# An attention and gated feed-forward block on one core: a projection's weights, a batch's values, and the third batch's turning and keys are done at other places in the slot order

## What is computed

```python
q = heads(concat([ssm_states, hidden], -1) @ Wq, 32)
k, v = heads(hidden @ Wk, 8), heads(hidden @ Wv, 8)
ssm_k, ssm_v = heads(ssm_states @ Wsk, 8), heads(ssm_states @ Wsv, 8)
scores = q @ concat([rep(ssm_k), rep(k)]).T / sqrt(16) + alibi
scores = where(window of 64 keys back, scores, -inf)
o = softmax(scores) @ concat([rep(ssm_v), rep(v)])
return o @ Wo
```

## Time and profile before

| | us |
|---|---|
| median of 3 runs | 875.04 (873.82 to 875.11) |
| the profiled execution | 874.93 |
| its span | 871.9 |
| PE busy, share of the span | 862.1 (99%) |
| DVE busy | 545.9 (63%) |
| ACT busy | 400.6 (46%) |
| POOL busy | 519.5 (60%) |

### The profile page before, as it was taken

The page is one execution under the profiler, slowest core; times in us unless marked ns, Lnnn a source line. Parts: engine busy times, 40 slices in busy tenths (PEclk is TensorE's granted clock), DMA queues, the critical chain, the costliest instruction groups (busy, mean ns, idle before and its releaser), DMA issues.

```text
span 871.9 us, 17392 instructions
## 1 busy us (share of the span) xinstructions
PE 862.1 (99%) x6662; PEld 754.0 (86%) x6662; DVE 545.9 (63%) x983; ACT 400.6 (46%) x810; POOL 519.5 (60%) x532
## 2 busy tenths in 40 slices
PE   9999999999999999999999999999999999999998
PEld 8889999999999999988888868888888888888886
DVE  7675666776666657755436746556655665565567
ACT  5754555554545545654034243444444444444431
POOL 3861443534335232353769998547888888788731
PEclk9999999999999999999999999999999999999999
DMA  8677576776868659630101345311212021121046
GB/s 275 170 142 185 149 200 192 188 197 162 210 164 219 164 138 261 140 98 26 49 24 53 106 147 163 139 50 48 72 50 73 25 72 56 42 73 48 1 137 249
DMA packets 76459, 108.07 MB, mean 124 GB/s; under 512 B 7249, under 2 KB 47954, under 8 KB 75346
## 3 DMA queue, kind: packets, MB, share of 16 engines
q1 hardware_dynamic: 74168, 105.94, 43.2%
q10 hardware_dynamic: 2210, 1.03, 0.4%
HBM read 70.71 MB, written 31.00 MB: 117 GB/s over the span
## 4 chain that ended last, share of the span: by engine, by line
PE 94%; DVE 2%; DMA 1%; issue 1%; ACT 0%; SPq 0%; DVEq 0%; ACTq 0%
PE ps_scores L2219 20%; PE ps_proj L1840 16%; PE ps_scoresT L2219 10%; PE ps_scoresT L1977 7%; PE ps_o L1991 6%; PE ps_proj L1829 6%; PE ps_scores L1950 5%; PE ps_scores L1840 5%; PE ps_proj L2219 5%; PE ps_proj L1898 5%; PE ps_scoresT L1840 4%; DMA xn_rows<-in_x 1%; PE ps_o_max L2018 1%; PE ps_o L1829 1%; PE ps_o_max L1829 1%; PE ps_o_max L1878 1%
## 5 line engine op out<-in xcount | busy, mean ns | idle before, releaser
L1127 ACT ACTIVATE probsT<-ps_scoresT 128x512 f32<-128x512 f32 (+1 forms) x256 | 138.9, 545 | 148.6 <-PE ps_scoresT L1977 144.1
L1485 DVE TENSOR_REDUCE neg_max<-ps_scores 128x2 f32<-128x384 f32 (+1 forms) x256 | 131.7, 517 | 108.1 <-PE ps_scores L1950 107.4
L1352 ACT ACTIVATE part_sums<-ps_scores 128x512 f32<-128x512 f32 x96 | 57.4, 598 | 132.5 <-PE ps_scores L2219 130.5
L1977 PE MATMUL ps_scoresT<-q_stack,k_stack 116*128 116x256 f32 x448 | 106.1, 307 | 0.0
L840 POOL TENSOR_TENSOR o_normal<-o_blocks,inv_sums 128x256 f32<-128x256 f32 x32 | 19.9, 622 | 137.0 <-DVE inv_sums L1506 137.0
L1950 PE MATMUL ps_scores<-k_stack,q_stack 114*128 114x192 f32 (+1 forms) x512 | 94.6, 267 | 2.9 <-DMA q_stack<-qT_hi 1.4
L1950 PEld LDWEIGHTS ps_scores<-k_stack,q_stack 114*128 114x128 f32 x512 | 83.0, 190 | 9.8 <-DMA q_stack<-qT_hi 2.0
L995 POOL TENSOR_TENSOR w_expert_lo<-w_sums,w_expert_hi 128x256 fp32r<-128x256 f32 x64 | 63.8, 1008 | 45.5 <-ACT w_expert_hi L1276 45.5
L1007 POOL TENSOR_TENSOR big<-big,basis 128x512 f32<-128x512 f32 x56 | 77.9, 1409 | 16.3 <-DVE basis L1779 16.3
L1977 PEld LDWEIGHTS ps_scoresT<-q_stack,k_stack 116*128 116x128 f32 x448 | 70.8, 190 | 3.8
L1770 DVE TENSOR_TENSOR basis<-part_sums,silu_gate 128x512 f32<-128x512 f32 x32 | 24.2, 756 | 67.3 <-ACT silu_gate L1360 67.3
(11 more groups left out here) (311 smaller groups left out, 2507.5 us busy)
## 6 DMA issues: line engine op xcount, KB each, us to landing
k_stack<-k_kept SPq DMA_DIRECT2D x64, 192.0 KB, 4.5
big<-coeff_rows SPq DMA_DIRECT2D x8, 1024.0 KB, 4.6
q_stack<-q_kept SPq DMA_DIRECT2D x40, 192.0 KB, 4.1
q_kept<-qT_hi SPq DMA_DIRECT2D x10, 512.0 KB
x_rows<-in_x SPq DMA_DIRECT2D x9, 512.0 KB, 6.6
k_kept<-kT_hi SPq DMA_DIRECT2D x16, 256.0 KB
x_kept<-x_rows SPq DMA_DIRECT2D x16, 256.0 KB, 2.8
w_raw<-in_L_ffn_w_gate SPq DMA_DIRECT2D x16, 256.0 KB, 2.9
```

The lines of the kernel that those rows point to most:

```text
L1127: act.activation(PT[:, g % 2, 2 * j:2 * j + blocks].rearrange("p h f r w -> p (h f r w)"), ST[:, n % 2, 0:blocks].rearrange("p h n -> p (h ...
L1352: act.activation(TP[:, u % 2, j, :], src[:, u % 2, :], ACT.Copy).then_inc(taken, 1)
L1485: dve.tensor_reduce(NM[:, g // 2 % 2, g % 2, 2 * i:2 * i + 2], SA[:, n % 2, :, 0:keys], AX.X, ALU.max, negate=True).then_inc(max_done, 1)
L1977: ins = pe.matmul(ST[:, n % 2, v, :], KS[0:ROWS, g, j + v, 1 - v].rearrange("p w s -> p (w s)"), QS[0:ROWS, g, j + v].rearrange("p f r w - ...
```

## The change

Output weights: SP loads the four quarters two by two, behind the stacks of the sixth head (number 5) and of the seventh (number 6), and the split goes from slots 12 to 15 to slots 18 to 21. The second batch's values go from 20, 21, 22 to 15, 16, 17. Of the third batch, the high halves of the context go from 22 and 23 to 19 and 20, the low ones from 28 to 22, turning from 23 and 27 to 20 and 22, keys from 31, 32, 33 to 24, 25, 28. Its row statistics go before slot 0 and its normalising to 14. The high part of the second batch's first queries is taken between two of ACT's `rows_out`, the low part in slot 2 in place of 8. The load of ACT's Exp table goes from before the slots to slot 11.

```diff
-EARLY_Q = ((-1, -1, 7), (-1, -1, 8), (9, 10, 11), (12, 13, 14))
+EARLY_Q = ((-1, -1, 1), (-1, -1, 8), (9, 10, 11), (12, 13, 14))
-EARLY_STATS = (11, 13)
+EARLY_NORMAL = 14
+EARLY_V, EARLY_PREP, EARLY_K, EARLY_CTX_HIGH = (15, 16, 17), (20, 22), (24, 25, 28), (19, 20)
-SPLIT_WO = 12
+SPLIT_WO, WO_AFTER = 18, {5: (0, 1), 6: (2, 3)}
+EARLY_CTX_LOW = 22
+EXP_TABLE = 11
...
+def early_due(n, early, usual, first, after=0):
+    if n == early + after:
+        return first
+    return due(n, usual + after, first + 1)
...
+def values_due(n, part, after=0):
+    return early_due(n, EARLY_V[part], V_PROJ[part], 1, after)
...
         keep_k(0)
-        for n in range(FIRST_O, len(halves)):
-            weight(n)
         for g in range(HK):
             stack_k(0, g)
             stack_q_first(g)
+            for n in WO_AFTER.get(g, ()):
+                weight(FIRST_O + n)
...
         k_high(1)
         rows_out(4)
+        q_high(1, 0)
         rows_out(6)
-        table_of(ACT.Exp)
...
+        for t in range(TB):
+            row_stats(2, t)
         for n in range(SLOTS):
```

More of the change, by code:

```diff
@@ L117, in queries_due, with normal_due, prep_due, keys_due @@
     return due(n, Q_PROJ[r][part] + after, 2)
-def stats_due(n, t):
-    return 2 if n == EARLY_STATS[t] else due(n, STATS[t], 3)
+def normal_due(n):
+    return 2 if n == EARLY_NORMAL else due(n, STATS[1] + 1, 3)
+def early_due(n, early, usual, first, after=0):
[4 more added lines that the diff above has]
+    return early_due(n, EARLY_V[part], V_PROJ[part], 1, after)
+def prep_due(n, t, after=0):
+    return early_due(n, EARLY_PREP[t], PREP[t], 2, after)
+def keys_due(n, part, after=0):
+    return early_due(n, EARLY_K[part], K_PROJ[part], 2, after)
+def ctx_low_due(n, j):
+    return 2 if n == EARLY_CTX_LOW else due(n, CTX_LOW[j], 3)
 def pair_due(n, offset):
@@ L197, in projections @@
     for n in range(SLOTS):
-        jobs = [("k", due(n, K_PROJ[0], 2), 0)] + [("q", queries_due(n, i, 0), i) for i in range(G)]
-        jobs += [("v", due(n, V_PROJ[0], 1), 0)]
+        jobs = [("k", keys_due(n, 0), 0)] + [("q", queries_due(n, i, 0), i) for i in range(G)]
+        jobs += [("v", values_due(n, 0), 0)]
         jobs += [("wo", batch_at(n, lambda b: wo_slots(b, t)[0]), t) for t in range(TB)]
@@ L209, in turns @@
     for n in range(SLOTS):
-        jobs = [("prep", due(n, PREP[t], 2), t) for t in range(TB)] + [("turn_v", due(n, TURN_V), 0)]
+        jobs = [("prep", prep_due(n, t), t) for t in range(TB)] + [("turn_v", due(n, TURN_V), 0)]
         jobs += [("x", batch_at(n, lambda b: x_turn_slot(b, t)), t) for t in range(TB)]
@@ L912, in _ @@
             for j in range(2):
-                b = due(n, CTX_LOW[j], 2)
+                b = ctx_low_due(n, j)
                 if b is not None:
                     ctx_low(b, j)
-            b = stats_due(n - 1, 1)
+            b = normal_due(n)
             if b is not None:
@@ L1209, in _ @@
             for i in range(2):
-                b = due(n, CTX_HIGH[i], 2)
+                b = early_due(n, EARLY_CTX_HIGH[i], CTX_HIGH[i], 2)
                 if b is not None:
                     ctx_high(b, i)
-                b = due(n, PREP[i] + 1, 2)
+                b = prep_due(n, i, 1)
                 if b is not None:
                     prep_high(b, i)
-            b = due(n, K_PROJ[2] + 1, 2)
+            b = keys_due(n, 2, 1)
             if b is not None:
@@ L1220, in _ @@
                 b = queries_due(n, i, 2, 1)
-                if b is not None:
+                if b is not None and (b > 1 or i > 0):
                     q_high(b, i)
+            if n == EXP_TABLE:
+                table_of(ACT.Exp)
             for t in range(TB):
@@ L1607, in _ @@
             for t in range(TB):
-                b = due(n, PREP[t] + 1, 2)
+                b = prep_due(n, t, 1)
                 if b is not None:
                     prep_low(b, t)
-            b = due(n, K_PROJ[2] + 1, 2)
+            b = keys_due(n, 2, 1)
             if b is not None:
@@ L1617, in _ @@
                     q_low(b, i)
-            b = due(n, V_PROJ[2] + 1, 1)
+            b = values_due(n, 2, 1)
             if b is not None:
@@ L1636, in _ @@
             for t in range(TB):
-                b = stats_due(n, t)
+                b = due(n, STATS[t], 3)
                 if b is not None:
@@ L2111, in _ @@
             for t in range(TB):
-                b = due(n, PREP[t], 2)
+                b = prep_due(n, t)
                 if b is not None:
@@ L2124, in _ @@
             for part in range(3):
-                b = due(n, K_PROJ[part], 2)
+                b = keys_due(n, part)
                 if b is not None:
@@ L2131, in _ @@
                         queries(b, r, part)
-                b = due(n, V_PROJ[part], 1)
+                b = values_due(n, part)
                 if b is not None:
```

## The result

The changed kernel takes 878.49 us (median of 14 executions, 876.97 to 885.19), the kernel before 875.25 us (14 executions, 873.45 to 878.5). The ratio is 1.0036, with a 95% interval of 1.0020 to 1.0052: slower by 0.36%, outside the forecast range, on the side to which I gave 0.22. The profiled execution took 878.26 us with a span of 875.4 us (874.93 and 871.9 before).

What follows compares the result with a forecast made beforehand. TensorE, 99% busy, bounds the kernel; only idle time before 70 us can change. Of 3.1 us won up to slot 18, 2.9 are given back in Scalar's and POOL's queues: gain 0.2, median 874.8 us, range 872.9 to 877.0.

Steps and rivals of the forecast that it cites:

- the start and the filled slots: Slots 0 to 18: earlier stacks 1.3 us, slot 9's wait gone 0.45, values in slots 15 to 17 1.35.
- I took 1.3: First stack load: lands 1.3 us earlier, bounds 0 to 2.0, with the weight loads no longer beside the keys' write.
- The rival that they land no earlier: Slot 0's stacks: the keys' write is not held up by the weights, 1.3 us less won, 876.0; no separate chance.
- its reading of the rule on how a write is spread over the DMA engines: Keys' write: spread over 8 of sixteen engines, so weights behind it hardly hold it up; the 1.3 us would be 0.
- the chain through Scalar, VectorE and POOL: Slots 18 to 24: Scalar tight, TensorE waiting for VectorE and POOL; 2.9 of 3.1 us won given back, nearly all there.
- about 2: Slot 24: the first key third waits for both context halves on POOL, about 2 us of TensorE's time.
- The slower rival: Third weight load 0.8 to 2 us late stops Scalar's in-order queue, shifting Exps and keys: 876.7 to 878, chance 0.22.
- the 0.2 us that I took for a late load: Third weight on Scalar: load at 55.6, wanted at 54.8, 0.8 us late; 0.2 us taken, moving slot 32 to 68.6.
- the four loads' long issue came from full rings: SP: the loads' 4.14 us issue blamed on full rings at the start, so 2.2 us taken at the new place.
- the second batch's stacks are not the bound: Slot 32: SP's chain frees it at 67.8 (66.8 to 70), before the 68.6 of the other chain.
- I had left 0.8 in slots 29 to 31: Slots 29 to 31 have no filler, so 0.8 of the present 1.0 us of waiting for row maxima stays.
- its end at 60.7 plus slot 25 with a third (1.5), slot 26 with the value product (2.15) …: Slots 24 to 28: from the first key third's end at 60.7, slots 25 to 28 summed to 66.2.

Runs made afterwards that it cites:

- e1: The changed kernel with only the output weights' part undone (loads ahead of the first stacks, split in slots 12 to 15): 875.44 us, ratio to before 0.9998.
- e5: The kernel before with only the second batch's values moved to slots 15 to 17: 874.62 us, ratio to before 0.9990.
- e10: The changed kernel with weights, turning, keys and context halves as before; early values and first queries' low part stay: 874.40 us, ratio 0.9990.
- e6: The changed kernel with the output weights split in slots 21 to 24 instead of 18 to 21: 875.84 us, ratio to before 1.0002.
- e9: The changed kernel with weight splits in slots 21 to 24 and both low context halves in slot 21, ahead of them on POOL: 874.54 us.
- e2: The changed kernel with 32 unused products added where TensorE waits, in slots 20, 22 and 24: 877.16 us, ratio to before 1.0028.
- e8: e6 with the third batch's key thirds in slots 25, 29 and 31 instead of 24, 25 and 28: 876.28 us, ratio to before 1.0011.
- e3: The kernel before with only the output weights' part (loads behind sixth and seventh heads, split in slots 18 to 21): 877.73 us, ratio 1.0025.

## Why the prediction was wrong, point by point

The places of the sum against the trace, 0.68 us taken off the measured ones:

| place | forecast | measured |
|---|---|---|
| first stack load behind the keys' write | 7.5 | 7.1 (28.12 − 21.02) |
| turn in slot 20 | 53.5 | 53.4 |
| third weight split on Scalar | 54.8, load 0.8 late | 54.8, load in time |
| turn in slot 22 | 56.5 | 56.7 |
| first key third in slot 24 | 59.7 (60.7 less 0.96) | 59.6 |
| both context halves done on POOL | 60.4 | 60.6 |
| second keys written | 52.9 | 53.6 |
| slot 32 | 68.6 | 71.3 |
| slot 34 | 69.6 | 72.4 |

- **Right: the start and the filled slots.** No wait at 9 and 17. The stacks started 1.7 us earlier behind the write than before (8.78 to 7.10), where I took 1.3. In the four profiles with the weights behind the write (before, e1, e5, e10) it is 8.74 to 8.81, in all others 7.06 to 7.14. The rival that they land no earlier fell, and with it its reading of the rule on how a write is spread over the DMA engines: the weights behind it held its landing up.
- **Right: the chain through Scalar, VectorE and POOL.** Every place up to slot 24 came within 0.2 us, and TensorE waited there for what I had named. One reading in it was off: the key third began with the first half of the context and not with both, so that the wait was 1.24 us and not "about 2"; the start that the sum used, 59.7, fits only this. The slower rival's mechanism, Scalar stopped by a load, didn't occur: in the changed kernel Scalar's operations followed each other within 0.1 us from 51.78 to 59.6, and the 0.2 us that I took for a late load were not needed. That the four loads' long issue came from full rings no run shows; at their new place the pairs took 1.05 us each on SP.
- **Right: the second batch's stacks are not the bound.** Slot 32 waited 0.76 us for VectorE's maxima, of which I had left 0.8 in slots 29 to 31.
- **Wrong: "its end at 60.7 plus slot 25 with a third (1.5), slot 26 with the value product (2.15) …".** These terms came from the earlier trace rows, where TensorE has 2.4 GHz. I had put three waits, in slots 20, 22 and 24, into the sum, counted each once, as idle time, and took the durations behind them from rows that stand behind no such waits. What the lower level cost is read from e6, which has the same order on TensorE and kept 1.00: the starts of the scores in slots 25, 26 and 27, first in the changed kernel, then in e6.

```profile
62.09 0.57 PE L1984 MATMUL ps_scores<-k_stack,q_stack 114*128 114x192 f32 x2
...
64.60 0.57 PE L1984 MATMUL ps_scores<-k_stack,q_stack 114*128 114x192 f32 x2
...
67.34 0.37 PE L1984 MATMUL ps_scores<-k_stack,q_stack 114*128 114x192 f32 x2
```

```profile
60.24 0.37 PE L1984 MATMUL ps_scores<-k_stack,q_stack 114*128 114x192 f32 x2
...
61.63 0.37 PE L1984 MATMUL ps_scores<-k_stack,q_stack 114*128 114x192 f32 x2
...
63.94 0.37 PE L1984 MATMUL ps_scores<-k_stack,q_stack 114*128 114x192 f32 x2
```

| stretch | forecast | e6, at 1.00 | the change |
|---|---|---|---|
| third in slot 24 | 0.96 | 1.04 (estimate: eight matmuls and a restart) | 1.84 |
| slot 25 | 1.5 | 1.39 | 2.51 |
| slot 26 | 2.15 | 2.31 | 2.74 |
| slots 27 and 28 | 1.92 | 2.14 | 2.15 |
| slots 29 to 31, with the wait at 32 | 2.2 | 2.51 | 2.50 |
| slots 32 and 33 | 0.95 | 1.13 | 1.12 |

  Slot 34 is 2.8 us late against the forecast (72.4 and 69.6). The clock made 2.4 of it, in the first three rows. The other terms were 0.8 short at any clock, most of it in slots 26 and 28 to 31; the load that was not late and a start of the third 0.1 earlier took 0.3 to 0.4 back.
- **In the median it is larger.** The forecast was 874.8, measured 878.49, 3.7 more; all 14 executions had 0.996 or less, 7 of them less than the profiled one's 0.996. Their mean clocks average 0.9946, which is 4.7 us of 875 if every lost cycle counts; at the profiled execution's rate (2.4 us lost where 6.8 us at 0.50 make 3.4) it is 3.3, an estimate. How much of the 3.7 is the clock's and how much are waits that vary can't be told apart further in executions without a trace. e9, which removes the wait of slot 24 and cuts that of slot 22 from 1.23 to 0.65, gives back 3.9.
- **The chances.** I gave the slower side 0.22 on a mechanism that did not happen. The profile of before showed no drop of the clock at all, so there was no row to price one; but the sum itself showed three waits within 8 us. A price for TensorE at the lower level from the first of them to the end of the last (53.5 to 60.7), half of 7.2 us, would have given 878.4. That it meets the measured time is luck: the drop that came lay elsewhere, from 58.1 to 64.9 on the same scale, so the stretch of the waits is no bound for it. The range should have gone beyond 877.0, by an amount that no row of before could give.

The Trainium skill (TensorE: Matmul & The Clock Gate, "HAM oscillation — how this bites in real kernels") describes waits after which the clock is at half rate, and puts the price at the throttled time times one half. By it the 6.8 us here cost 3.4 us. The rows give 2.4. For one thing, 1.2 us of the stretch was the wait of slot 24, in which there was nothing to slow down, and by the same rule the 5.56 busy us cost 2.8. For another, the projection matmuls stood 0.21 us apart, not twice 0.12. The trace agrees in kind, and the page's price is an upper end here.

## What to carry to other kernels

When a sum puts several waits on TensorE close together, price the matmuls behind them at the lower clock too, and look at the row of the granted clock before looking for a cause elsewhere. When work is moved into an in-order queue, write down the order in every queue that it passes: here it decided between 878.5 and 874.5 us whether the four weight splits stood ahead of the context halves in Scalar's and POOL's queues or behind them, and the DMA transfers, to which much of the forecast's text went, were not the loss. Filler products in front of a wait are a cheap test of whether the waits bring the clock down, if the same number of them is also run where TensorE doesn't wait; count the executions that keep the clock, since the times of the two also differ by what the idle time hides.

## What the runs showed of the hardware

**The clock fell at a wait pattern, not at a wait.** The longest wait ahead of the drop was 1.23 us, with TensorE busy 6.21 of 8.80 us; the wait of slot 24 came behind it. e2's profiled execution had one of 1.84 us and kept 1.00 there. e1's fell at 38.0, behind a wait of 2.0 us for the first stacks. e6 was busy only 5.99 of the same 8.80 us:

```profile
50.00:58.80 8.80, 5.99 (x50) 5.41 (x48) 6.52 (x13) 7.19 (x15) 2.72 (x3) 1.00 0.85 180
```

It kept 1.00 in that execution and lost it in 8 of 11. The kernel before lost some in 15 of 108. So one execution says little, and kernels have to be compared by how many of their executions keep the clock. What decides in a single one is left open.

**A VectorE operation of 0.17 us takes up to 1.19 us beside POOL.** POOL's timeline in e8, and VectorE's:

```profile
57.20 2.50 POOL L863 TENSOR_TENSOR actT_lo<-ctx_turned,actT_hi 128x512 fp32r<-128x512 f32 x2
59.66 2.50 POOL L901 TENSOR_TENSOR wo_lo<-wo_stage,wo_hi 128x512 fp32r<-128x512 f32 x2
```

```profile
58.01 0.49 DVE L1525 CAST max_halves<-neg_max 128x16 fp32r<-128x16 f32 x1
58.54 1.19 DVE L1527 TENSOR_TENSOR max_halves<-neg_max,max_halves 128x16 fp32r<-128x16 f32 x1
```

POOL's first half ends at 58.45, the second at 59.70 (half of the 2.50 each); VectorE's two operations end at 58.50 and 59.73, each with one of POOL's. The changed kernel has it too (0.77 and 1.19 at 59.37 and 60.17), hidden there behind TensorE's slow third. The Trainium skill (SBUF — State Buffer, "SBUF: two separate sides") says that GpSimd and certain VectorE operations, among them those with two inputs in SBUF, take a shared pair of ports by an exclusive lock, held for a whole instruction. The trace agrees in kind: each of the two ends with an operation of POOL's. Not every VectorE operation is held: in the kernel before, the row maxima at 46.69 took 0.56 us beside POOL's 2.54, as long as without it. My sum had no such term; it is what makes POOL's work before slot 25 cost TensorE 1.67 us in e3 and 1.90 in e8.
